# Values times output weights computed ahead of the key transposes, and the first scores of grouped attention ahead of the second queries

## The reference, cut to what matters

```python
# layer 2, feed-forward: 8 experts, 2 of them for each token
for e in range(8):
    combine_w = where(topk_idx == e, topk_weight, 0).sum(-1)
    y = y + combine_w[:, None] * ((silu(xf @ gate_proj[e].T) * (xf @ up_proj[e].T)) @ down_proj[e].T)
# layer 3, attention: 16 query heads of 64, 4 key and value heads
Q, K, V = rope(ln(x) @ Wq), rope(ctx @ Wk), ctx @ Wv       # K and V repeated over 4 query heads each
attn = softmax(Q @ K.T / 8 + rel_pos_bias, axis=-1)
x = x + (attn @ V).reshape(2, 1024, 1024) @ Wo
```

## Time and profile before

| | us |
|---|---|
| median of 3 runs | 1065.18 |
| lowest and highest | 1063.49, 1068.7 |
| the profiled execution | 1073.24 |
| its span | 1071.4 |
| keys of layer 3 start on PE | 486.75 |
| first transpose of the expert blocks | 522.02 |
| last product of `keep_warm` ends | 602.94 |
| first transposes of attention weights (tile 0) | 633.30 |

### The profile page before, as it was taken

How to read it: one execution, slowest core, us unless ns; L and a number is a source line. 1 busy time by engine, 2 the same in 40 slices (tenths; PEclk the granted TensorE clock), 3 DMA queues, 4 the chain that set the end, 5 groups by cost and what they waited for, 6 DMA issues and landing times. The chain is left out here.

```text
span 1071.4 us, 17147 instructions
## 1 busy us (share of the span) xinstructions
PE 906.0 (85%) x5755; PEld 646.2 (60%) x5755; DVE 741.2 (69%) x1709; ACT 376.4 (35%) x856; POOL 385.1 (36%) x283
## 2 busy tenths in 40 slices
PE   3899979999899967864799689999998409999987
PEld 2677744444577755632478357777776207777776
DVE  5788857989688869776477689999875622243133
ACT  2466540000255547731355143434333203122212
POOL 1566503333466724246155223333332140111111
PEclk9899989999989997967899999999999759999999
DMA  5000079999200009012365641111110762633200
GB/s 171 1 1 0 1 234 292 314 328 327 101 1 1 0 8 252 1 51 95 98 196 162 217 138 48 48 48 48 48 48 1 246 218 80 196 108 132 87 11 18
DMA packets 87257, 117.14 MB, mean 109 GB/s; under 512 B 12464, under 2 KB 75949, under 8 KB 86781
## 3 DMA queue, kind: packets, MB, share of 16 engines
q1 hardware_dynamic: 77455, 88.15, 27.2%
q10 hardware_dynamic: 4408, 15.46, 4.3%
q0 software_dynamic: 5328, 12.70, 3.3%
HBM read 68.08 MB, written 50.16 MB: 110 GB/s over the span
## 5 line engine op out<-in xcount | busy, mean ns | idle before, releaser
L925 PE MATMUL psum<-m_W,lnT 128*128 128x512 f32 x256 | 114.3, 598 | 0.0
L405 POOL TENSOR_TENSOR prob<-prob,a_rden 128x1232 f32<-128x1232 f32 x32 | 71.9, 2248 | 80.0 <-DVE a_rden L477 80.0
L925 PEld LDWEIGHTS psum<-m_W,lnT 128*128 128x128 f32 x256 | 47.2, 190 | 58.3 <-issue 57.0
L2210 PE MATMUL psum<-g_VW,pT 128*128 128x256 f32 (+1 forms) x320 | 73.4, 384 | 1.6 <-ACT pT L2129 1.6
L2688 PE MATMUL psum<-x_xT,x_w 128*128 128x320 f32 x256 | 72.2, 441 | 1.5 <-DVE x_xT L2495 1.5
L910 POOL TENSOR_TENSOR m_masked<-m_rel,m_mrow 128x1232 f32<-128x1232 f32 x16 | 42.9, 2684 | 77.5 <-DMA masked_bias<-m_masked 60.3
L2366 POOL DMA_INDIRECT out_x<-x_yt,x_X x20 | 19.7, 985 | 140.5 <-DVE x_yt L2509 139.9
L2210 PEld LDWEIGHTS psum<-g_VW,pT 128*128 128x128 f32 (+1 forms) x320 | 59.5, 190 | 12.6 <-ACT pT L2129 5.1
L1968 POOL TENSOR_TENSOR prob<-prob,g_rden 128x1232 f32<-128x1232 f32 x16 | 36.0, 2248 | 83.9 <-DVE g_rden L2066 83.9
L2688 PEld LDWEIGHTS psum<-x_xT,x_w 128*128 128x128 f32 x256 | 49.2, 194 | 22.9 <-issue 4.2
L1965 POOL TENSOR_TENSOR g_qr<-g_t 128x1024 f32<-128x1024 f32 x16 | 37.7, 2357 | 70.5 <-DVE g_t L2036 70.5
(11 more groups left out here) (445 smaller groups left out, 2076.7 us busy)
## 6 DMA issues: line engine op xcount, KB each, us to landing
routed_rows<-hole SPq DMA_DIRECT2D x8, 2210.0 KB, 33.9
masked_bias<-m_masked ACTq DMA_DIRECT2D x16, 616.0 KB, 7.8
g_bias<-masked_bias SPq DMA_DIRECT2D x16, 616.0 KB, 3.8
x_w<-in_L_ffn_w SPq DMA_DIRECT2D x16, 512.0 KB, 4.7
x_w<-in_L_ffn_w SPq DMA_DIRECT2D x8, 1024.0 KB, 8.2
m_xb<-routed_rows SPq DMA_DIRECT2D x39, 130.0 KB
m_rel<-in_rel_bias ACTq DMA_DIRECT2D x8, 616.0 KB, 10.3
expert_rows<-hole SPq DMA_DIRECT2D x1, 4680.0 KB, 35.8
```

Of the source, the lines that this page charges most:

```text
L405: nc.gpsimd.tensor_tensor(heads(c.prob[b]), heads(c.prob[b]), rden[b][:, :].unsqueeze(2).to_broadcast([P, H, SK]), ALU.mult).then_inc(norm ...
L925: last = nt.matmul(c.ps[p][:, :], c.lnT[b][:, k * P:(k + 1) * P], W[:, k, p * 512:(p + 1) * 512], start=(k == 0), stop=(k == KC - 1))
L2210: last = nt.matmul(bank_y[:, 0:D], c.pT[b][0:w, j * P:(j + 1) * P], VW[0:w, b, j, :], start=(j == 0), stop=(j == NB - 1))
```

## The change

The products `VW` move ahead of the transposes of the keys on PE and go through three banks (1, 2 and 3) one at a time; ACT alone copies all 16; PE waits for `VT`, for the weights and for `slot_ok` = 2 before the first. The transposes of the keys of batch 0 go to bank 4. Behind them PE runs 36 products of no use (`keep_warm`) and then waits for the copies of `VW` and of the keys. In grouped attention SP loads the results of group j + 2 ahead of `VW` of batch j; for tiles 0 and 1 DVE adds the halves of the rotation instead of POOL; on PE `queries(1)` stands behind `scores(0)` instead of behind `q_transpose(0)`; on DVE `shift(0)` stands ahead of `rope(1)`.

```diff
--- before.py
+++ after.py
@@ -1040,13 +1040,14 @@
     VWs = [c.lnk[0:SK, :].rearrange("k (h n) -> k h n", h=HB),
            c.lnT_all[0:SK, :, :].rearrange("k a (h n) -> k (a h) n", n=D)]
     vw_dram = c.vw_dram
-    bank_k, bank_vT, bank_kT = c.ps[0], [c.ps[1], c.ps[2]], [c.ps[3], c.ps[0]]
+    bank_vw = [c.ps[1], c.ps[2], c.ps[3]]
+    bank_k, bank_vT, bank_kT = c.ps[0], [c.ps[1], c.ps[2]], [c.ps[4], c.ps[0]]
-             "hid_ok", "hT_ps", "hT_ok", "y_ps", "y_ok", "ne_ok", "idx_ok", "g_in", "k_ps", "vT_ps", "vT_ok", "kr_ok", "krT_ps", "vw_ps", "vwa_ok", "vwd_ok",
+             "hid_ok", "hT_ps", "hT_ok", "y_ps", "y_ok", "ne_ok", "idx_ok", "g_in", "k_ps", "vT_ps", "vT_ok", "kr_ok", "krT_ps", "vw_ps", "vw_ok", "kb_ok",
              "vw_out", "pz_ok", "hm_ok")
     x_in = [sem(c, f"m_x_in{k}") for k in range(RING)]
     y_out = [sem(c, f"m_y_out{k}") for k in range(YR)]
@@ -1092,8 +1093,7 @@
         early = [sp.value_load(row0[0:1, b:b + 1], min_val=0, max_val=XROWS - P) for b in range(4)]
 
         def store_values(n):
-            sp.wait_ge(s["vwa_ok"], n + 1)
-            sp.wait_ge(s["vwd_ok"], n + 1)
+            sp.wait_ge(s["vw_ok"], 2 * n + 2)
             h = slice(4 * (n % 4), 4 * (n % 4) + 4)
             sp.dma_start(vw_dram[n // 4].rearrange("(h k) n -> k h n", k=SK)[:, h, :], VWs[n // 4][:, h, :]
                          ).then_inc(s["vw_out"], 16)
@@ -1453,11 +1453,7 @@
             chain(nv.tensor_tensor(a2[b][:, :, hd:DH], k[:, :, 0:hd], row(c.gSn[0:SK, 0, hd:DH]), ALU.mult))
             for o in range(2):
                 nv.tensor_tensor(KR[:, b, :, o, :], a1[b], a2[b], ALU.add).then_inc(s["kr_ok"], 1)
-        for n in range(8):
-            dve.wait_ge(s["vw_ps"], n + 1)
-            h = 4 * (n % 4) + 1
-            nv.tensor_copy(VWs[n // 4][:, h:h + 3:2, :],
-                           c.ps[5 + 2 * (n % 2)][0:SK, :].rearrange("k (a n) -> k a n", a=2)).then_inc(s["vwd_ok"], 1)
+
         def hidden(b):
             k = b % 2
             scale = xb[:, b % RING, D + 2:D + 3]
@@ -1642,19 +1638,19 @@
         for j in range(2):
             na.activation(VT[:, 2 * j:2 * j + 2, :].rearrange("p g n -> p (g n)"), bank_vT[j][:, 0:2 * B * SK], ACT.Copy
                           ).then_inc(s["vT_ok"], 1)
+        for n in range(8):
+            h = 4 * (n % 4)
+            for o in range(2):
+                act.wait_ge(s["vw_ps"], 2 * n + o + 1)
+                na.activation(VWs[n // 4][:, h + o:h + o + 3:2, :],
+                              bank_vw[(2 * n + o) % 3][0:SK, :].rearrange("k (a n) -> k a n", a=2), ACT.Copy
+                              ).then_inc(s["vw_ok"], 1)
         act.wait_ge(s["hm_ok"], 1)
         for b in range(B):
             act.wait_ge(s["krT_ps"], b + 1)
             for o in range(2):
                 na.activation(c.gKB[:, b, :, o, :], bank_kT[b][:, 0:G * SK].rearrange("p (g k) -> p g k", k=SK), ACT.Identity,
-                              scale=hmask_scaled[:, o:o + 1])
-
-        for n in range(8):
-            act.wait_ge(s["vw_ps"], n + 1)
-            h = 4 * (n % 4)
-            na.activation(VWs[n // 4][:, h:h + 3:2, :],
-                          c.ps[4 + 2 * (n % 2)][0:SK, :].rearrange("k (a n) -> k a n", a=2), ACT.Copy
-                          ).then_inc(s["vwa_ok"], 1)
+                              scale=hmask_scaled[:, o:o + 1]).then_inc(s["kb_ok"], 1)
         bT_copy(0)
         bT_copy(1)
         for t in range(NB2 + 1):
@@ -1851,27 +1847,27 @@
                                  Wv3[:, k, g, :, :].rearrange("p r e -> p (r e)"), c.ctxT[:, k, :],
                                  start=(k == 0), stop=(k == KC - 1))
         last.then_inc(s["vT_ps"], 1)
+        pe.wait_ge(s["vT_ok"], 2)
+        pe.wait_ge(s["g_in"], 16 * 5)
+        pe.wait_ge(s["slot_ok"], 2)
+        for n in range(8):
+            b, m = n // 4, n % 4
+            for o in range(2):
+                rows = slice(o * DH, (o + 1) * DH)
+                wait(pe, s["vw_ok"], 2 * n + o - 2)
+                nt.matmul(bank_vw[(2 * n + o) % 3][0:SK, :], VT[rows, m, b * SK:(b + 1) * SK],
+                          Wo3[rows, 2 * m:2 * m + 2, :].rearrange("p a n -> p (a n)"), start=True, stop=True).then_inc(s["vw_ps"], 1)
         for b in range(B):
             pe.wait_ge(s["kr_ok"], 2 * B if b else 2)
             for g in range(G):
                 last = nt.transpose(bank_kT[b][:, g * SK:(g + 1) * SK], KR[:, b, g, :, :].rearrange("k r e -> k (r e)"),
                                     c.ident[0:SK, 0:SK])
             last.then_inc(s["krT_ps"], 1)
+        pe.wait_ge(s["wm_ok"], 4 * KC)
         pe.wait_ge(s["table_ok"], 1)
-        pe.wait_ge(s["wm_ok"], 4 * KC)
-        pe.wait_ge(s["vT_ok"], 2)
-        pe.wait_ge(s["g_in"], 16 * 5)
-        for n in range(8):
-            b, m = n // 4, n % 4
-            wait(pe, s["vwa_ok"], n - 1)
-            wait(pe, s["vwd_ok"], n - 1)
-            for o in range(2):
-                rows = slice(o * DH, (o + 1) * DH)
-                last = nt.matmul(c.ps[4 + 2 * (n % 2) + o][0:SK, :], VT[rows, m, b * SK:(b + 1) * SK],
-                                 Wo3[rows, 2 * m:2 * m + 2, :].rearrange("p a n -> p (a n)"), start=True, stop=True)
-            last.then_inc(s["vw_ps"], 1)
-        pe.wait_ge(s["vwa_ok"], 8)
-        pe.wait_ge(s["vwd_ok"], 8)
+        keep_warm(c, c.ps[5], 36)
+        pe.wait_ge(s["vw_ok"], 16)
+        pe.wait_ge(s["kb_ok"], 2 * B)
 
         def transpose(b):
             k = b % RING
@@ -1943,10 +1939,10 @@
     def _(sp):
         for j in range(2):
             sp.dma_start(bias[j][:, :], c.mb_dram[j * P:(j + 1) * P, :]).then_inc(bias_in[j % 2], 16)
+            expert_results(c, sp, j + 2)
             sp.dma_start(VW[:, j, 0:NB - 1, :], c.vw_dram[j, 0:(NB - 1) * P, :].rearrange("(j p) n -> p j n", p=P)
                          ).then_inc(s["vw_in"], 16)
             sp.dma_start(VW[0:LASTB, j, NB - 1, :], c.vw_dram[j, (NB - 1) * P:HB * SK, :]).then_inc(s["vw_in"], 16)
-            expert_results(c, sp, j + 2)
         expert_results(c, sp, 4)
         for j in range(2, NT):
             sp.wait_ge(s["s_used"], j - 1)
@@ -1958,7 +1954,7 @@
 
         def step(t, q):
             b = q % 2
-            if inside(t + 1):
+            if inside(t + 1) and t + 1 >= 2:
                 i = t + 1
                 pool.wait_ge(s["roped"], i + 1)
                 wait(pool, s["qT_ps"], i * 2)
@@ -2035,6 +2031,10 @@
             nv.tensor_tensor(a2[:, :, 0:half], qview[:, :, half:DH], bch(sn[:, ds(o, half)]), ALU.mult)
             nv.tensor_tensor(a2[:, :, half:DH], qview[:, :, 0:half], bch(sn[:, ds(o + half, half)]),
                              ALU.mult).then_inc(s["roped"], 1)
+            if i < 2:
+                wait(dve, s["qT_ps"], i * 2)
+                dve.wait_ge(s["roped"], i + 1)
+                nv.tensor_tensor(qr[:, :], t1[:, :], t2[:, :], ALU.add).then_inc(s["rope_ok"], 1)
 
         links = Chain(dve, s["links"])
 
@@ -2069,9 +2069,11 @@
 
         def step(t, q):
             b = q % 2
+            if t == 0:
+                shift(t, q)
             if inside(t + 1):
                 rope(t + 1, 1 - b)
-            if inside(t):
+            if inside(t) and t > 0:
                 shift(t, q)
             if inside(t + 7):
                 add_experts(range(4, 7) if t < 0 else (t + 7,))
@@ -2215,6 +2217,8 @@
             b = q % 2
             if inside(t):
                 scores(t, b)
+            if t == 0:
+                queries(1, 1)
             if inside(t - 1):
                 if is_static(t) and t == 1:
                     pe.wait_ge(s["vw_in"], 16 * 2 * B)
@@ -2227,7 +2231,7 @@
                 output(t - 1, 1 - b)
             if inside(t + 1):
                 q_transpose(t + 1, 1 - b)
-            if inside(t + 2):
+            if inside(t + 2) and t != -1:
                 queries(t + 2, b)
         for t in range(-2, NT + 1):
             step(t, t % 4)
```

## The result

| | before | after |
|---|---|---|
| median of 20 runs, us | 1064.37 | 1067.43 |
| lowest and highest | 1061.85, 1069.32 | 1066.11, 1070.91 |
| ratio to before, 95% interval | | 1.0026 [1.0014, 1.0038] |
| profiled execution (its span) | 1073.24 (1071.4) | 1067.07 (1065.3) |

The change costs 2.8 us (0.0026 of 1064.37), where 4.3 us less had been forecast. Against the profiled executions alone it looks like a gain: 1073.24 became 1067.07, close to the 1068.9 that the sum gave for it. But the profiled execution of before lies 3.9 us above the slowest of its own 20 runs. That surplus decides what the first half of the change is worth.

What follows compares the result with a forecast made beforehand. PE was taken to set the end in the expert blocks and from 619 to 660. -6.8 + 0 + 2.5 = -4.3 us takes the median from 1065.18 to 1060.9, range 1056.5 to 1065.5.

Steps and rivals of the forecast that it cites:

- the sum: Whole program: -6.8 for `VW`, 0 for grouped attention, 2.5 for the clock, -4.3 us together; profiled execution 1068.9.
- the `VW` products, -6.8 us: Opening of the expert blocks: earlier products let the first block transpose start when its load lands, 6.8 us earlier.
- (c): Rival, expert blocks' opening: clock falls under `VW` products, `keep_warm` runs at half clock, total 0: 1065 us; chance 0.17.
- (d): Rival, expert blocks' opening: half-clock products make the first transpose 4.3 us later, +6.8 in all: 1072 us; chance 0.06.
- first block transpose at 515.2: Sign, start of the expert blocks: first transpose at 515.2 with PE waiting for a DMA.
- Grouped attention at an even clock: Opening of grouped attention: earlier `scores(0)` is used up on DVE, `prob_transpose(0)` at 633.4 instead of 633.30, worth 0.
- The clock: 2.5 us: Opening of grouped attention: `scores(0)` in the half-clock stretch and a second fall behind 4.3 us idle cost 2.5 us.
- called the same: Total: a result within about 0.5%, 5.3 us, which a measurement cannot tell from before; chance 0.54.

Runs made afterwards that it cites:

- before again: The kernel of before, unchanged, run and profiled once more: ratio 0.9991, median 1063.82 us, profiled execution 1062.86 us.
- the two filled ones: The changed kernel, and its grouped attention half alone, each with 12 and 14 useless products in PE's two idle stretches: ratios 1.0000 and 1.0003.
- `VW` part alone: Kernel of before with only the moved `VW` products, three banks, ACT copying and 36 useless products: ratio 0.9997, median 1064.17 us.
- after filled: Changed kernel with 12 useless products ahead of `q_transpose(0)` and 14 ahead of `q_transpose(1)`: ratio 1.0000, median 1063.16 us.
- `VW` part filled: Kernel of before with the `VW` change, old grouped attention order, 16 and 8 useless products ahead of `q_transpose(0)` and `q_transpose(1)`: ratio 0.9995, median 1063.93 us.
- grouped attention alone: Kernel of before with only the grouped attention changes (SP order, DVE addition, new PE and DVE order): ratio 1.0028, median 1069.26 us.
- the mix: Changed kernel with PE's and DVE's old grouped attention order, keeping the `VW` change, SP's order and DVE's addition: ratio 1.0008.

## Why the prediction was wrong, point by point

**The step that failed: the `VW` products, -6.8 us.** It read "the block is there at some 515.1 and waits 6.9 us for PE" from the earlier trace rows. In that execution it was so, and the forecast for it (1068.9) met what the changed kernel's profile took (1067.07). The sum was then taken off the median, as if the 6.9 us were in every execution. They were not: in before again the block waits 0.4 us, and of the seven profiles with the products in their old place only this one has the long wait (beside the one in which 24 products were put there). The sign was in the table ahead of the prediction: the profiled execution took 1073.24 us, and the slowest of the runs shown 1068.7. The prediction named the 8 us of difference and did not ask where they were. They were in this wait: against the profiled execution of before again (1062.86), which is 10.4 us shorter, 9.2 us stand at the first block transpose (522.02 against 512.86) and 10.5 at the last down product (592.77 against 582.31 by the start of its pair), since the expert blocks began at the half clock (their first gate and up product took 2.07 us instead of 1.13). With -0.4 in place of -6.8, the same sum gives +2.1; measured were +2.8 by the ratio. (That 1065.18 + 2.1 = 1067.3 comes so near the measured 1067.43 is in part luck: 1065.18 was the median of 3 executions, that of 20 is 1064.37.)

**Its mechanics were right.** Products from 492.99 to 502.88 (forecast 491.5 to 502.3), a copy every 0.59 us (0.6 forecast), useless products ended at 511.3 (511.8), the transpose waits for a DMA. The clock stayed full, as was said against (c) and (d). The mark "first block transpose at 515.2" was nearly met, too (514.04), and says nothing: a time of the span compared with an execution that is 8 us off.

**Grouped attention at an even clock: 0 was forecast, and no loss beyond the spread of the profiles is measured** (50.11 against 49.47 and 50.40). DVE's addition took 1.23 us (1.2 forecast) and `scores(0)` came 4.9 to 5.1 us earlier (4.3). `q_transpose(1)` came later by 0.9 to 1.85 us at an even clock (32.66 against 31.73 and 30.81) where 0.95 was forecast. That maxima and additions of DVE eat the gain was right.

**The clock: 2.5 us forecast, 2.2 to 2.4 us measured**, and the place was right: scores in the low stretch and a second fall behind 3.93 us of idleness (4.3 forecast). It is shown and not only argued, since filling those idle stretches takes the fall and the loss away. The Trainium skill, "TensorE: Matmul & The Clock Gate", Part 4 (PE-mode transpose), says that transposes do not count as the engine being busy in the same way as products. By it the fall around `q_transpose(1)` was all but certain. There it fell in both profiles of the changed kernel and in the two of the new order with the old `VW` (with and without DVE's addition), and in neither of the two filled ones. This agrees with the rule, but plain idleness would do the same: no run here had transposes alone in place of the useless products, and the two are not told apart.

**The rivals and the range.** (c), "the first half gives little", came nearest (1065) by the wrong cause: it let the clock fall under the products, where what was missing was the wait itself. No rival said "this wait is in the profiled execution and not in the others". The 0.26% lie within the 0.5% that was called the same, for which 0.54 had been given. The range ended at 1065.5, 1.9 us short; its upper end rested on (c), whose 0 still counted up to 1.5 us won and a product stretch 0.8 us shorter against that one execution.

**What stays open.** Why that execution was late. Its trace shows where. DVE stood idle six times, 2.8 us together, between the instructions that work out the slots (lines 1330 to 1337), which in before again follow one another without a gap. Timelines of DVE, first the profile shown, then before again:

```profile
486.93 0.23 DVE L1330 TENSOR_TENSOR m_slotm<-psum,m_pre 128x64 f32<-128x64 f32 x1 [0.66 <-DVE m_pre L1327]
487.63 0.22 DVE L1331 TENSOR_TENSOR m_slotm<-m_slotm,m_base 128x64 f32<-128x64 f32 x1 [0.48 <-DVE m_slotm L1330]
```

```profile
485.85 0.23 DVE L1330 TENSOR_TENSOR m_slotm<-psum,m_pre 128x64 f32<-128x64 f32 x1
486.12 0.23 DVE L1331 TENSOR_TENSOR m_slotm<-m_slotm,m_base 128x64 f32<-128x64 f32 x1
```

So the corrections of the expert weights began 3.1 us later (495.19 against 492.06), and POOL's scatters were held 2.67 us for the slots. Then the products took 6 us more: they ran at 0.50 up to 508.7 and again from 512.2, with an idle time of 2.45 us in their midst. What made DVE pause, and whether the rest follows from it, was not tried; neither came back in the six later profiles with the products in that place. Nor is it known what the longest unprofiled executions hold: some of 1070.8 to 1072.2 us are among those of before, and one of 1071.48 among those of the `VW` part alone, in which no product stands right ahead of the block.

Also open is where the filled kernels lose what their opening wins: from the last output product of grouped attention to the end of the program it is 239.2 us in before again, 239.6 in after, 241.0 in after filled and 240.4 in the `VW` part filled. But it is 240.4 in grouped attention alone, too, which is not filled. These are single profiles, and no run was made on that.

## What to carry to other kernels

Before a wait is priced, set the profiled execution's time against the range of the other runs: where it lies outside, as 1073.24 did here, the surplus is somewhere in the trace, and a long wait that the change removes is the first suspect. A second profile of the same kernel settled it here: 0.4 us of wait in place of 6.9. Read then what would end last if the late engine were in time (here the scatters and the load behind them, 0.4 us away), and give "the wait is in this execution only" a chance of its own. Taking work from one idle stretch of TensorE to bring another forward can open a longer one (3.93 us here in place of 2.63), and what then falls into a half-clock stretch takes twice as long (scores 4.47 us in place of 2.26): 12 and 14 useless products in the two idle stretches were worth 4.3 us of opening here, and brought the program back to the time of before. A difference of under 1 us between two single profiles is not yet a cost.

## What the runs showed of the hardware that was not expected

An idle time of TensorE does not by its length alone tell whether the clock falls: behind 2.63 us (before, again, ahead of `q_transpose(1)`) it held, in the mix it went to 0.50 for 3.4 us just behind an idle time of 2.06 us, and in three profiles it fell under `queries(0)`, ahead of which PE had idled 1.22 to 1.28 and 0.47 us, while behind 2.00 and 0.47 us in before again it held there.

Sixteen products of depth 64 with neighbours on different halves of the rows went through three banks with one copying engine in 9.89 us, all at the full clock. The 9.73 us of before again, through four banks with two copying engines, are not like it: for 4.4 us of them PE ran at the half clock. Windows of before again, columns as in the earlier trace rows:

```profile
500.20:505.20 5.00, 5.00 (x16) 1.71 (x15) 1.37 (x2) 2.21 (x5) 3.78 (x5) 0.51 0.27 98
505.20:508.20 3.00, 2.97 (x16) 0.81 (x12) 1.89 (x3) 1.71 (x3) 2.39 (x3) 1.00 0.35 125
```

At the full clock that arrangement gave four products every 1.96 us (DVE's copies start at 506.58, 508.54 and 510.50), 0.49 each. So three banks with ACT alone, at 0.62 each, are the slower way; here it costs nothing, since PE waits for the block behind them.
